# Perceiver block on one core: a cross product in two column tiles, its code sums on GpSimd

## The chip, the cores and the metric

The kernel runs on one core of a Trainium2 chip. The core has five engines that run side by side and wait for each other through semaphores: TensorE (PE, matrix products, with weight loads on their own track PEld), VectorE (DVE), ScalarE (ACT), GpSimd (POOL) and SyncE (SP, which here issues the DMAs). The metric is the device time of one execution in microseconds (us). The kernel before takes 621.97 us, the median of three runs (621.82 to 622.06).

## The reference

Sixteen batches of 64 rows of 1024 numbers pass through three residual steps. The first is the one that the change touches:

```
x = x + matmul(fake_quant(layernorm(x), s1, z1), fake_quant(ctx, s2, z2))   # ctx: 16 x 1024 x 1024
x = x + attention(layernorm(x))      # qkv, 32 heads, rope, causal softmax, output projection
x = x + ffn(layernorm(x))            # x W^T + bias + a sum of 16 low-rank updates
fake_quant(x, s, z) = (clip(round(x / s + z), 0, 255) - z) * s
```

With codes q1 and q2 (0 to 255) the product is s1 s2 times the sum over k of (q1 - z1)(q2 - z2). The kernel feeds TensorE q1 - 128 on one side and 1024 + q2 on the other, both exact in 16-bit floats. Two corrections remain: one per row of x, and one per column of ctx, which is (128 - z1) times the column's sum of codes.

## The kernel before

Two batches make a pair of 128 rows, so there are eight pairs. Pairs follow each other, and the cross product of pair i + 1 is worked into the attention of pair i. `next_pair` stands once for each engine (ACT, DVE, PE) and holds that engine's instructions for one such step in the order in which the engine runs them; pairs 2 to 5 or 6 run it in a loop, `first_pair` (pair 0), pair 1 and pair 6 or 7 are written out. No scheduler moves anything. Each engine works its own list in order, so an instruction that waits holds all that is behind it on that engine.

The ctx of a pair comes in 16 chunks of 128 x 1024 numbers (`CHUNKS`), chunk c being batch c // 8 and slice c % 8 of k. SP loads chunk c into one of three slots (`slots`: two of `raw`, and `lnt`), and it may load chunk c when chunk c - 3 has been read (`load_chunk`). ACT turns a chunk into codes (`quantise`): it writes the low bytes of a 16-bit tile in a ring of six (`code`, `RING`), whose high bytes were set once to the 1024. It waits until PE has used the chunk that had the slot (`s_cmm`). PE multiplies (`chunk`): the weights are 128 columns, 64 of q1 - 128 for this batch and 64 of ones (`q1t`), the streamed operand is 512 columns of codes, twice per chunk. So rows 0 to 63 of the bank pair `XX` hold the product of one batch and rows 64 to 127 the sums of its codes. DVE adds both to x with four instructions of 64 x 1024 per pair (`cross_evac`, two per batch, once after chunk 7 and once after chunk 15), then normalises (`norm2`); PE transposes the result (`x_turn`), which starts the next pair.

The places at which PE runs chunks, scores, transposes and the projection are the dictionaries in `next_pair`: `qkv(i, 1, {6: [at(c, 0)]})` runs chunk 0 after the seventh of eight steps of the second qkv block, each step being three products of 128 x 512. GpSimd issues the load of the rows after next (`rows_after_next`), does one addition of 128 x 1024, and is otherwise idle.

Of the kernel before, what the change touches and what calls it, by code (L numbers as in the profile page):

```python
# [36 lines left out]
RAW, RING = 2, 6  # L37
# [6 lines left out]
I32, U8T = mybir.dt.int32, mybir.dt.uint8  # L44
# [9 lines left out]
def build(nc, x, ctx_in, consts, qkv_w, out_w, bias_rows, out_bias, ffn_wt, ffn_bias, lora_a, lora_b, lora_w, out):  # L54
# [6 lines left out]
    with es:  # L61
# [14 lines left out]
        q1t = sb("q1t", [P, KC, 2, 2, SEQ], F16)  # L76
# [17 lines left out]
        qc = sb("qc", [P, 6], F32)  # L94
# [28 lines left out]
        d16 = pr[:, 0, :].bitcast(F16)  # L123
        s1, z1 = cst[:, C_SCAL:C_SCAL + 1], cst[:, C_SCAL + 1:C_SCAL + 2]
# [10 lines left out]
        q1v = q1t[:, :, :, :, :].rearrange("p k b h t -> p (k b h t)")  # L135
# [3 lines left out]
        lora_stage = [raw[:, 0, :], raw[:, 1, :], q1v.bitcast(F32), lnt[:, :]]  # L139
        wt_lnt = lnt[:, :].rearrange("p (u n) -> p u n", u=2)  # L140
        yn_h = [xn_h[:, :, :], q1v[:, 0:DM].rearrange("p (k t) -> p k t", k=KC)]
        yn_l = [xn_l[:, :, :], q1v[:, DM:2 * DM].rearrange("p (k t) -> p k t", k=KC)]
# [12 lines left out]
        s_ones = sem("s_ones")  # L155
# [28 lines left out]
        s_cmm = sem("s_cmm")  # L184
        s_clast = sem("s_clast")
# [125 lines left out]
        def _(act):  # L311
# [20 lines left out]
            def quantise(i, c):  # L332
# [25 lines left out]
            def a_high(i, e):  # L358
                act.wait_ge(s_at, 2 * i + e + 1)
                act.activation(q1t[:, 4 * e:4 * e + 4, :, 0, :],  # L360
                               code_bank(i, e)[:, :].rearrange("p (k b t) -> p k b t", k=4, b=2), ACT.Copy).then_inc(s_ah, 1)
# [7 lines left out]
            def v_evac(i, n):  # L369
                act.wait_ge(s_qkv, 6 * i + 5 + n)  # L370
                act.activation(vv[:, n * NT:(n + 1) * NT], D[n][:, :], ACT.Copy, scale=1.0 / (XSC * WSC)).then_inc(s_v, 1)

# [24 lines left out]
            def lora_high(n):  # L397
                act.wait_ge(s_lora[n], 16)
                if n == 0:
                    act.wait_ge(s_cmm, CHUNKS * PAIRS)  # L400
# [14 lines left out]
            def first_pair():  # L415
# [22 lines left out]
                exponent(0, 1)  # L438
                q(5, 6, 7, 8)
# [21 lines left out]
            def next_pair(i, more, late=False):  # L461
# [21 lines left out]
                q(7, 8)  # L483
                w(28)
                qk_evac(i, 1)
                q(9)
                w(29)
                q(10, 11)
                exponent(i, 0)
                q(12)  # L490
                exponent(i, 1)
                qk_evac(i, 2)
                q(13)
# [8 lines left out]
                q(14)  # L502
                w(31)
                if late:
                    v_evac(i, 0)
                    q(15)
                    exponent(i, 2)
                else:
                    exponent(i, 2)
# [83 lines left out]
        def _(sp):  # L593
            def load_chunk(i, c):
                if isinstance(i, int) and i == 0 and c == CHUNKS - 1:
                    for n in range(2):
                        sp.dma_start(chunk0_stage(c)[:, n, :], ctx_v[0, c // KC, c % KC, :, n * NT:(n + 1) * NT]).then_inc(s_clast if n else s_ctx0[c], 16)
# [1152 lines left out]
```

## Time and profile before

| | |
|---|---|
| median of the runs | 621.97 us |
| span of the profiled execution, from its first to its last instruction | 620.4 us |
| PE busy | 601.3 us (97%) |
| DVE busy | 472.8 us (76%) |
| ACT busy | 292.3 us (47%) |
| POOL busy | 11.5 us (2%) |
| one step of the pair loop, from one x_turn to the next | 58.25 us |

The span lies 1.57 us under the median of the runs; this is what lies around the span. A matmul's printed duration (0.38 us) holds its latency too. In a stream the starts stand 0.2155 us apart, and this spacing is what a product costs. Times in the rows are us from the start of the span; a bracket at a row's end is the time that the engine stood idle before it, and who ended that.

### The profile page before, as it was taken

The page shows a single profiled execution, that of the slowest core. Times are in us where ns is not written, and L with a number is a line of the kernel's source. Part 1 is how long each engine was busy: PE and PEld are TensorE (multiplying, and loading weights), DVE is VectorE, ACT ScalarE, POOL GpSimd, SP SyncE. Part 2 cuts the span into 40 slices and gives each one's busy share as a digit, 9 for nine tenths or more (in the row PEclk, how much of TensorE's full clock was granted, in tenths as well). Part 3 has the DMA queues.
Part 4 walks back from the last instruction along what each step waited for, and adds up shares of the span by engine and source line. Part 5 has one row for each costly group of instructions (what it writes and reads, how often), then busy time and mean ns, then how long its engine had stood idle before and what let it go on. Part 6 is the DMA issues. An engine that isn't in the chain of part 4 may idle for free.

```text
span 620.4 us, 12885 instructions
## 1 busy us (share of the span) xinstructions
PE 601.3 (97%) x4937; PEld 310.6 (50%) x4937; DVE 472.8 (76%) x938; ACT 292.3 (47%) x366; POOL 11.5 (2%) x17
## 2 busy tenths in 40 slices
PE   3898999999999999999999999999999999999998
PEld 1463454455455545554555455545545554454455
DVE  6899998788659965987596769659964789867661
ACT  5887695865464546534644554464431243110010
POOL 3000010000000000000000000000000000000000
PEclk9999999999999999999999999999999999999999
DMA  8999995861464175226712671464241042232311
GB/s 319 387 386 361 388 365 205 277 208 69 165 220 161 69 254 193 95 81 258 266 71 97 207 237 68 161 217 130 102 136 35 1 172 102 85 119 85 114 55 53
DMA packets 38912, 108.14 MB, mean 174 GB/s; under 512 B 3802, under 2 KB 4186, under 8 KB 38880
## 3 DMA queue, kind: packets, MB, share of 16 engines
q1 hardware_dynamic: 37744, 104.35, 47.5%
q0 software_dynamic: 992, 3.18, 1.5%
q8 instruction: 21, 0.34, 0.2%
q10 hardware_dynamic: 144, 0.18, 0.2%
q14 instruction: 11, 0.09, 0.0%
HBM read 99.30 MB, written 8.39 MB: 174 GB/s over the span
## 4 chain that ended last, share of the span: by engine, by line
PE 84%; DVE 5%; SPq 4%; DMA 4%; ACT 1%; issue 1%; ACTq 0%; DVEq 0%
PE dense L1259 16%; PE dense L1261 16%; PE dense L1260 16%; PE cross L1308 7%; PE turn L1250 6%; PE dense L1426 4%; PE dense L1427 4%; PE dense L1428 4%; DVE wq L860 4%; PE score L1387 2%; SPq L600 2%; DMA wq<-in_qkv_w 2%; PE score L1413 2%; DMA raw<-in_ctx 2%; PE dense L1442 1%; PE cross L1473 1%
## 5 line engine op out<-in xcount | busy, mean ns | idle before, releaser
L1259 PE MATMUL dense<-wq,xn_h 128*128 128x512 f16 x400 | 151.9, 380 | 0.0
L1260 PE MATMUL dense<-wq,xn_h 128*128 128x512 f16 x400 | 151.6, 379 | 0.0
L1261 PE MATMUL dense<-wq,xn_l 128*128 128x512 f16 x400 | 151.6, 379 | 0.0
L351 ACT ACTIVATE code<-raw,cst,qc 128x1024 uint8<-128x1024 f32 x72 | 87.7, 1235 | 6.7 <-DMA raw<-in_ctx 6.5
L1308 PE MATMUL cross<-code,q1t 128*128 128x512 f16 x256 | 73.4, 387 | 3.0 <-DVE xa L867 1.4
L1261 PEld LDWEIGHTS dense<-wq,xn_l 128*128 128x128 f16 x400 | 39.1, 98 | 47.2
L1259 PEld LDWEIGHTS dense<-wq,xn_h 128*128 128x128 f16 x400 | 39.1, 98 | 41.5 <-issue 1.6
L1260 PEld LDWEIGHTS dense<-wq,xn_h 128*128 128x128 f16 x400 | 39.2, 98 | 38.2
L351 ACT ACTIVATE code<-lnt,cst,qc 128x1024 uint8<-128x1024 f32 x32 | 39.6, 1239 | 28.4 <-DMA lnt<-in_ctx 25.4
L906 DVE SCALAR_TENSOR_TENSOR at<-cst,score 128x512 f32<-128x512 f16 x24 | 16.4, 683 | 37.4 <-PE score L1387 37.2
L1426 PE MATMUL dense<-wo,rope 128*128 128x512 f16 x112 | 42.5, 379 | 0.0
L1428 PE MATMUL dense<-wo,rope 128*128 128x512 f16 x112 | 42.4, 379 | 0.0
L1427 PE MATMUL dense<-wo,rope 128*128 128x512 f16 x112 | 42.4, 379 | 0.0
L1308 PEld LDWEIGHTS cross<-code,q1t 128*128 128x128 f16 x256 | 24.6, 99 | 33.8 <-ACT code L351 4.3
L367 ACT ACTIVATE at<-turn 128x512 f32<-128x512 f32 x32 | 19.0, 593 | 47.2 <-PE turn L1250 34.1
L381 ACT ACTIVATE at<-turn 128x512 f32<-128x512 f32 x32 | 19.1, 596 | 35.6 <-PE turn L1250 35.5
L375 ACT ACTIVATE at<-at 128x512 f32<-128x512 f32 x32 | 19.9, 624 | 32.2 <-DVE at L912 32.2
L892 DVE TENSOR_TENSOR rope<-dense,cst 128x512 f32<-128x512 f32 x32 | 22.0, 687 | 10.3 <-PE dense L1261 8.3
L943 DVE SCALAR_TENSOR_TENSOR xa<-dense,xa 128x512 f32<-128x512 f32 x16 | 11.0, 689 | 18.1 <-PE dense L1428 18.1
L387 ACT ACTIVATE rope<-score 128x256 f16<-128x256 f32 x28 | 9.2, 381 | 29.8 <-PE score L1413 29.8
L898 DVE TENSOR_TENSOR rope<-rope 128x512 f32<-128x512 f32 x32 | 22.1, 692 | 1.5
L920 DVE TENSOR_TENSOR at<-at,ssum 128x512 f32<-128x512 f32 x32 | 22.1, 692 | 1.1
(204 smaller groups left out, 992.6 us busy)
## 6 DMA issues: line engine op xcount, KB each, us to landing
raw<-in_ctx SPq DMA_DIRECT2D x72, 512.0 KB, 4.5
lnt<-in_ctx SPq DMA_DIRECT2D x32, 512.0 KB, 4.2
wo<-in_ctx SPq DMA_DIRECT2D x16, 512.0 KB, 8.6
wo<-in_qkv_w SPq DMA_DIRECT2D x12, 512.0 KB, 11.7
wq<-in_qkv_w SPq DMA_DIRECT2D x8, 512.0 KB, 11.9
x_scratch<-xa SPq DMA_DIRECT2D x8, 512.0 KB, 3.0
wq<-x_scratch SPq DMA_DIRECT2D x8, 512.0 KB, 3.7
wq<-in_ctx SPq DMA_DIRECT2D x7, 512.0 KB, 11.7
```

What stands on the lines that cost most here:

```text
L351: act.activation(low_bytes, src, ACT.Identity, scale=qc[:, 1:2], bias=z2).then_inc(s_u8, 1)
L860: dve.scalar_tensor_tensor(lo, staged(j), WSC, hi, ALU.mult, ALU.subtract).then_inc(s_wlo, 1)
L898: dve.tensor_tensor(rope[:, 2 + j % 2, :], rope[:, 0, :], rope[:, 1, :], ALU.add).then_inc(s_qr, 1)
L920: dve.tensor_tensor(p3, p3, ssum[:, g % 2, :].unsqueeze(2).to_broadcast([P, HPG, SEQ]), ALU.mult).then_inc(s_p, 1)
L1250: ins = pe.transpose(bank[:, k * P:(k + 1) * P], src[:, c:c + P], ident)
L1259: pe.matmul(bank[:, :], a_h[:, k, :], w_hi, start=(k == 0 and not started), stop=False)
L1260: pe.matmul(bank[:, :], a_h[:, k, :], w_lo, start=False, stop=False)
L1261: ins = pe.matmul(bank[:, :], a_l[:, k, :], w_hi, start=False, stop=(k == KC - 1 and not last))
L1308: ins = pe.matmul(X[n][:, :], lhs, code[:, c % RING, n * NT:(n + 1) * NT], start=(kc == 0), stop=(kc == KC - 1))
L1426: pe.matmul(D[n][:, :], c_h[:, k, :], wo_h[:, k, cols], start=(k == 0), stop=False)
L1427: pe.matmul(D[n][:, :], c_h[:, k, :], wo_l[:, k, cols], start=False, stop=False)
L1428: ins = pe.matmul(D[n][:, :], c_l[:, k, :], wo_h[:, k, cols], start=False, stop=(k == KC - 1))
```

## The change

- The products. PE no longer has columns of ones in the weights. For each slice kc of k it loads 64 columns of q1 - 128 per batch and runs the two batches as two matmuls into the two halves of the same bank (rows 0 to 63 and 64 to 127), first for columns 0 to 511, then for the others (`cross`). A chunk is now slice c // 2 of batch c % 2.
- The sums of codes. GpSimd adds each chunk's codes, as 32-bit integers that hold two codes each, to one of two accumulators (`add_codes`, 16 additions of 128 x 512 per pair). DVE casts both to 16-bit floats (`sums_as_f16`), and PE multiplies them by 128 - z1, as two 16-bit parts, in eight products into the same banks (`cross_shift`). For pair 0 PE takes the codes themselves with that shift (`first_cross`, six products more per slice).
- The addition to x. DVE reads each bank once, 128 x 512, two instructions per pair (`cross_evac`).
- The ring holds eight chunks. A slot is free when both PE and GpSimd have used it.
- The load of the rows after next is issued by ACT. The order in ACT's list and PE's list is written anew.

The core of the diff:

```diff
-RAW, RING = 2, 6
+CODE_SUM = -0x20032000
+RAW, RING = 2, 8
...
-                taken = CHUNKS * i + c - (CHUNKS % RING - 1 if c < CHUNKS % RING else RING - 1)
+                taken = CHUNKS * i + c - (RING - 1)
                 if above(taken):
                     act.wait_ge(s_cmm, taken)
+                if above(taken - CHUNKS):
+                    act.wait_ge(s_acc, taken - CHUNKS)
...
+            def add_codes(i, *cs):
+                for c in cs:
+                    pool.wait_ge(s_u8, CHUNKS * i + c + 1)
+                    if c < 2:
+                        pool.wait_ge(s_cbank, 2 * i)
+                        before = acc_from[:, :].to_broadcast([P, NT])
+                    else:
+                        pool.wait_ge(s_acc, CHUNKS * i + c - CHUNKS - 1)
+                        before = acc_words[:, c % 2, :]
+                    pool.tensor_tensor(acc_words[:, c % 2, :], code[:, c % RING, :].bitcast(I32), before, ALU.add).then_inc(s_acc, 1)
...
-                link(dve.scalar_tensor_tensor(x_rows(i)[rows, :], XX[0:SEQ, :], qc[0:SEQ, 2:3], x_rows(i)[rows, :], ALU.mult, ALU.add))
-                dve.scalar_tensor_tensor(x_rows(i)[rows, :], XX[SEQ:P, :], qc[SEQ:P, 2:3], x_rows(i)[rows, :], ALU.mult, ALU.add).then_inc(s_ce, 1)
+            def sums_as_f16(i):
+                dve.wait_ge(s_acc, CHUNKS * i)
+                dve.tensor_copy(acc[:, :], acc[:, :].bitcast(U16T)).then_inc(s_accf, 1)
+            def cross_evac(i, n):
+                dve.wait_ge(s_cbank, 2 * i + n + 1)
...
+                dve.scalar_tensor_tensor(x_rows(i)[:, cols], X[n][:, :], qc[:, 2:3], x_rows(i)[:, cols], ALU.mult, ALU.add).then_inc(s_ce, 1)
...
+            def cross(i, *ks):
+                for kc in ks:
...
+                    pe.wait_ge(s_u8, CHUNKS * i + 2 * kc + 2)
+                    for n in range(2):
+                        for b in range(2):
+                            ins = pe.matmul(X[n][b * SEQ:(b + 1) * SEQ, :], q1t[:, kc, b, :],
+                                            code[:, (2 * kc + b) % RING, n * NT:(n + 1) * NT], start=(kc == 0), stop=False)
+            def cross_shift(i):
+                pe.wait_ge(s_accf, i)
+                for n in range(2):
+                    for part in range(2):
+                        for b in range(2):
+                            ins = pe.matmul(X[n][b * SEQ:(b + 1) * SEQ, :], shift[:, part:part + 1].to_broadcast([P, SEQ]),
+                                            acc_sums[:, b, n * NT:(n + 1) * NT], start=False, stop=(part == 1))
...
-                    qkv(i, 1, {2: [at(codes)], 5: [at(codes_turned, 0), at(qk_turn, i, 0), at(m, 0)], 6: [at(c, 0)], 7: [at(c, 1)]})
+                    qkv(i, 1, {2: [at(codes)], 5: [at(codes_turned, 0), at(qk_turn, i, 0), at(m, 0)]})
...
-                    qkv(i, 4, {1: [at(turned, i, 2), at(p_turn, i, 0)], 4: [at(qk_turn, i, 3)], 6: [at(scores, i, 1)], 7: [at(p_turn, i, 1), at(c, 8, 9)]})
+                    qkv(i, 4, {1: [at(turned, i, 2), at(p_turn, i, 0)], 4: [at(qk_turn, i, 3)], 6: [at(scores, i, 1)], 7: [at(p_turn, i, 1), at(c, 4, 5)]})
...
-                qkv(i, 5, {1: [at(c, 10, 11), at(m, 4)], 2: [at(c, 12, 13), at(m, 5)], 3: [at(c, 14, 15), at(values_due, i, 0)], 4: [at(values, i, 0)],
-                           6: [at(evacuated, i, 0), at(p_turn, i, 2)], 7: [at(p_turn, i, 3)]})
+                qkv(i, 5, {1: [at(m, 4)], 2: [at(m, 5)], 3: [at(c, 6, 7), at(values_due, i, 0)], 4: [at(values, i, 0)],
+                           6: [at(shifted), at(evacuated, i, 0), at(p_turn, i, 2)], 7: [at(p_turn, i, 3)]})
```

In PE's new order slices 0 and 1 stand behind the first scores of the step, slices 2 and 3 in the fourth qkv block, 4 and 5 at the end of the fifth, 6 and 7 in the sixth.

ACT's list, in the copy of `next_pair` for pair 6 (the loop has the same order). `code<-` are the quantisations, `at<-at` the exponents of the softmax, `at<-turn` with `s_qkt` the copies of transposed q and k, `at<-turn` with `s_pt` the copies of transposed probabilities. Before, from chunk 12 of the next pair to its chunk 15:

```order
L351 ACTIVATE code<-raw,cst,qc 128x1024 [waits s_cmm,s_slot0]
L375 ACTIVATE at<-at 128x512 [waits s_sub]
L367 ACTIVATE at<-turn 128x512 [waits s_qkt]
L351 ACTIVATE code<-raw,cst,qc 128x1024 [waits s_cmm,s_slot1]
L381 ACTIVATE at<-turn 128x512 [waits s_pv,s_pt]
L367 ACTIVATE at<-turn 128x512 [waits s_qkt]
L381 ACTIVATE at<-turn 128x512 [waits s_pv,s_pt]
L351 ACTIVATE code<-lnt,cst,qc 128x1024 [waits s_cmm,s_slot2]
L375 ACTIVATE at<-at 128x512 [waits s_sub]
L351 ACTIVATE code<-raw,cst,qc 128x1024 [waits s_cmm,s_slot0]
L375 ACTIVATE at<-at 128x512 [waits s_sub]
```

Now, from the same exponent on (chunks 11, 12, 13, 14 and 15):

```order
L389 ACTIVATE at<-at 128x512 [waits s_sub]
L376 ACTIVATE at<-turn 128x512 [waits s_qkt]
L360 ACTIVATE code<-lnt,cst,qc 128x1024 [waits s_acc,s_cmm,s_slot2]
L395 ACTIVATE at<-turn 128x512 [waits s_pv,s_pt]
L376 ACTIVATE at<-turn 128x512 [waits s_qkt]
L395 ACTIVATE at<-turn 128x512 [waits s_pv,s_pt]
L360 ACTIVATE code<-raw,cst,qc 128x1024 [waits s_acc,s_cmm,s_slot0]
L360 ACTIVATE code<-raw,cst,qc 128x1024 [waits s_acc,s_cmm,s_slot1]
L360 ACTIVATE code<-lnt,cst,qc 128x1024 [waits s_acc,s_cmm,s_slot2]
L389 ACTIVATE at<-at 128x512 [waits s_sub]
L360 ACTIVATE code<-raw,cst,qc 128x1024 [waits s_acc,s_cmm,s_slot0]
L389 ACTIVATE at<-at 128x512 [waits s_sub]
```

Chunks 12 and 13 have moved behind the second copy of transposed probabilities; before, only 14 and 15 stood there.

DVE's list in the loop, from the third softmax to the rows that the projection needs (`at<-at,ssum` is a finished softmax, `rope<-score,rope` the low part of the attention's output). Now:

```order
L938 TENSOR_TENSOR at<-at,ssum 128x512 [waits s_dv]
L891 REGISTER_ALU
L892 CAST acc<-acc 128x2048 [waits s_acc]
L936 TENSOR_REDUCE ssum<-at 128x8 [waits s_exp]
L787 REGISTER_ALU
L937 RECIPROCAL ssum<-ssum 128x8 [waits s_dv]
L787 REGISTER_ALU
L938 TENSOR_TENSOR at<-at,ssum 128x512 [waits s_dv]
L896 REGISTER_ALU
L900 SCALAR_TENSOR_TENSOR xb<-cross,qc,xb 128x512 [waits s_cbank]
```

The cast, which waits for GpSimd's last addition, stands ahead of the fourth softmax; before, nothing stood between the third and the fourth.

## Rows read from the trace of the kernel before

**Rows 1.** The page: its span and the busiest engine.

```profile
span 620.4 us, 12885 instructions
PE 601.3 (97%) x4937; PEld 310.6 (50%) x4937; DVE 472.8 (76%) x938; ACT 292.3 (47%) x366; POOL 11.5 (2%) x17
```

**Rows 2.** Windows, loop step and pair 1: length, then PE, PEld, DVE, ACT, POOL busy.

```profile
276.00:334.25 58.25, 58.25 (x533) 30.12 (x532) 44.13 (x89) 29.23 (x36) 0.53 (x1) 1.00 0.46 162
...
103.28:159.28 56.00, 55.96 (x521) 28.62 (x519) 45.32 (x76) 37.00 (x45) 0.58 (x1) 1.00 0.51 170
```

**Rows 3.** PE's timeline in one loop step: start us, us, line, instruction, count.

```profile
292.02 0.61 PE L1250 MATMUL turn<-cst,rope 128*128 128x128 f32 x4
...
293.11 0.59 PE L1308 MATMUL cross<-code,q1t 128*128 128x512 f16 x2
293.54 0.38 PE L1259 MATMUL dense<-wq,xn_h 128*128 128x512 f16 x1
...
315.15 0.38 PE L1261 MATMUL dense<-wq,xn_l 128*128 128x512 f16 x1
315.46 1.16 PE L1387 MATMUL score<-at 32*64 32x64 f32 x64
...
317.21 0.60 PE L1250 MATMUL turn<-cst,at 128*128 128x128 f32 x4
...
322.83 1.03 PE L1308 MATMUL cross<-code,q1t 128*128 128x512 f16 x4
...
324.43 0.86 PE L1413 MATMUL score<-at 64*32 64x64 f32 x64
...
328.20 0.38 PE L1426 MATMUL dense<-wo,rope 128*128 128x512 f16 x1
```

**Rows 4.** ACT's timeline in the same loop step.

```profile
280.68 1.24 ACT L351 ACTIVATE code<-lnt,cst,qc 128x1024 uint8<-128x1024 f32 x1 [2.93 <-DMA lnt<-in_ctx]
...
317.85 0.60 ACT L381 ACTIVATE at<-turn 128x512 f32<-128x512 f32 x1 [2.98 <-PE turn L1250]
318.34 1.23 ACT L351 ACTIVATE code<-lnt,cst,qc 128x1024 uint8<-128x1024 f32 x1
...
319.99 1.23 ACT L351 ACTIVATE code<-raw,cst,qc 128x1024 uint8<-128x1024 f32 x1
```

**Rows 5.** SP's timeline: the issue of the load that ACT awaits at 280.68.

```profile
277.35 0.33 SPq L622 DMA_DIRECT2D lnt<-in_ctx  x1
```

**Rows 6.** DVE's timeline: a 16-bit scaling at the start, then the loop step.

```profile
25.41 0.48 DVE L1099 TENSOR_SCALAR rope<-rope,cst 128x1024 f16<-128x1024 f16 x1
...
285.31 0.16 DVE L783 SCALAR_TENSOR_TENSOR nw<-nw 128x1 f32<-128x1 f32 x1
...
291.22 0.69 DVE L898 TENSOR_TENSOR rope<-rope 128x512 f32<-128x512 f32 x1
...
323.94 0.69 DVE L920 TENSOR_TENSOR at<-at,ssum 128x512 f32<-128x512 f32 x1
324.67 1.28 DVE L866 SCALAR_TENSOR_TENSOR xb<-cross,qc,xb 64x1024 f32<-64x1024 f32 x1
...
327.30 0.76 DVE L936 SCALAR_TENSOR_TENSOR rope<-score,rope 128x256 f16<-128x256 f32 x2
```

**Rows 7.** GpSimd's one addition (POOL's timeline), and DVE beside it.

```profile
81.29 2.36 POOL L747 TENSOR_TENSOR xa<-xa,outb 128x1024 f32<-128x1024 f32 x1 [7.43 <-DVE at L920]
...
81.45 1.27 DVE L866 SCALAR_TENSOR_TENSOR xb<-cross,qc,xb 64x1024 f32<-64x1024 f32 x1 [0.33 <-PE cross L1308]
```

**Rows 8.** PE's timeline at the end of pair 0: the last chunk and x_turn.

```profile
94.83 0.60 PE L1308 MATMUL cross<-code,q1t 128*128 128x512 f16 x2 [0.26 <-ACT code L351]
...
103.12 1.04 PE L1250 MATMUL turn<-cst,lnt 128*128 128x128 f32 x8
```

**Rows 9.** DVE's and ACT's timelines at the start: last addition to x, first copy after x_turn.

```profile
32.22 0.76 DVE L878 SCALAR_TENSOR_TENSOR xa<-cross,qc,xa 64x512 f32<-64x512 f32 x1
...
38.91 1.07 ACT L355 ACTIVATE xn_h<-turn 128x512 f16<-128x512 f32 x2
```

More of the change, by code:

```diff
@@ L747, in _ @@
             pool.tensor_tensor(xa[:, :], xa[:, :], outb[:, :], ALU.add).then_inc(s_cp, 1)
-            with pool.Fori(1, PAIRS - 2) as i:
-                rows_after_next(i)
+            add_codes(1, *range(12, CHUNKS))
+            with pool.Fori(2, PAIRS) as i:
+                add_codes(i, *range(CHUNKS))
             pool.wait_ge(s_st, 16 * PAIRS)
@@ L813, in row_codes @@
                 dve.wait_ge(s_a, i + 1)
-                link(dve.tensor_scalar(rs1[:, :], rs1[:, :], qc[:, 3:4], qc[:, 4:5], ALU.mult, ALU.add))
+                constant = qc[:, 4:5] if isinstance(i, int) and i == 0 else qc[:, 6:7]
+                link(dve.tensor_scalar(rs1[:, :], rs1[:, :], qc[:, 3:4], constant, ALU.mult, ALU.add))
             def out_base(i):
@@ new lines, in cross_shift, with first_cross @@
+            def cross_shift(i):
+                pe.wait_ge(s_accf, i)
+                for n in range(2):
+                    for part in range(2):
+                        for b in range(2):
+                            ins = pe.matmul(X[n][b * SEQ:(b + 1) * SEQ, :], shift[:, part:part + 1].to_broadcast([P, SEQ]),
+                                            acc_sums[:, b, n * NT:(n + 1) * NT], start=False, stop=(part == 1))
+                    ins.then_inc(s_cbank, 1)
+            def first_cross(kc):
+                if kc == 0:
+                    pe.wait_ge(s_ah, 2)
+                pe.wait_ge(s_u8, 2 * kc + 2)
+                for n in range(2):
+                    if n and kc == KC - 1:
+                        pe.wait_ge(s_u8half, 2)
+                    for part in range(3):
+                        for b in range(2):
+                            lhs = q1t[:, kc, b, :] if part == 0 else shift[:, part - 1:part].to_broadcast([P, SEQ])
+                            ins = pe.matmul(X[n][b * SEQ:(b + 1) * SEQ, :], lhs, code[:, (2 * kc + b) % RING, n * NT:(n + 1) * NT],
+                                            start=(kc == 0 and part == 0), stop=(kc == KC - 1 and part == 2))
+                            if n and part == 2 and (b or kc < KC - 1):
+                                ins.then_inc(s_cmm, 2 if kc == KC - 1 else 1)
+                            elif part == 2 and kc == KC - 1 and b != n:
+                                ins.then_inc(s_cbank, 1)
@@ L1540, in first_pair, with c @@
             def first_pair():
-                def c(*cs):
-                    for n in cs:
-                        chunk(1, n)
+                def c(*ks):
+                    cross(1, *ks)
                 def rows_high(k):
@@ L1579, in next_pair, with c, shifted @@
             def next_pair(i, ahead):
-                def c(*cs):
-                    for n in cs:
-                        if ahead:
-                            chunk(i + 1, n)
+                def c(*ks):
+                    if ahead:
+                        cross(i + 1, *ks)
+                def shifted():
+                    if ahead:
+                        cross_shift(i + 1)
                 def m(u):
@@ L1628, in _ @@
             next_codes(0)
-            pe.wait_ge(s_ones, 1)
-            for n in range(CHUNKS):
-                chunk(0, n)
-                if n < KC:
-                    constants(16 if n == KC - 1 else 3)
+            for kc in range(KC):
+                first_cross(kc)
+                if kc < KC - 1:
+                    constants(6)
             next_codes(1)
```

151 lines of the change are left out of this document (71 added, 80 removed).

## The prediction

> **What bounds the kernel now.** I read first the page's busy shares: PE has something in flight for 601 of 620.4 us [rows 1]. That alone doesn't say that PE is the bound, so I read next the windows of one loop step: PE is busy for all of its 58.25 us, and for 55.96 of pair 1's 56.00 [rows 2]. Five of the eight pairs run such a step, so in the body of the kernel what leaves PE's list leaves the time, as long as nobody else becomes late. The third reading is therefore how close the others are, in the timelines of PE, ACT and DVE for one step [rows 3, 4, 6]. ACT sleeps 2.98 us before the copy at 317.85, since it waits for PE's transposition; its last code of the next pair starts at 319.99 and ends at 321.22, 1.6 us before PE takes chunks 14 and 15 (322.83). DVE ends the low part of the attention's output at 328.06, and PE's projection starts at 328.20. So ACT's margin for the last code is 1.6 us, and DVE's before the projection is 0.1.
>
> **The products.** A chunk costs PE 293.54 - 293.11 = 0.43 us [rows 3], sixteen cost 6.9 a pair. Now 32 matmuls run as 16 pairs of column tiles. If a pair costs one spacing of 0.2155, that is 3.45, and the eight shift products 0.86. That two column tiles with different streams do overlap, rows 3 bear out: at 324.43, 64 products of 64 f32 columns, in 2 row groups and 4 column groups, take 0.86 us. The four f32 transpositions of 128 columns at 292.02 are printed with 0.61, of which 0.17 is latency (a product's 0.38 less its spacing): 0.11 each. So 64 f32 columns cost 0.055, and one after another these 64 would take 3.5. Two row groups explain a factor of 2, the observed one is 4. Each change between full and tiled products costs a gap: scores start 0.31 after the product ahead of them (315.15 to 315.46), 0.1 over the spacing. Five tiled groups a step make 0.5. PE's list thus shrinks by 6.9 - 3.45 - 0.86 - 0.5 = 2.05 us a step. This is what a step would gain if nothing became late.
>
> The Trainium skill (TensorE: Matmul & The Clock Gate, Part 3) has three column tiles at 2.38 times one, 0.79 of the ideal; by that, as an estimate, a pair would cost 0.27 instead of 0.2155 and the sum below would rise by some 4 us.
>
> **The addition to x.** Four DVE instructions of 1.28 to 1.29 go (5.2 us a step, [rows 6]), two of 128 x 512 (0.69 at 291.22, some 0.65 from start to start) and the cast come: DVE has less to do.
>
> **GpSimd's additions.** One of 128 x 1024 takes 2.36 [rows 7]; half the columns, 1.2. Sixteen make 19 of 58 us, so GpSimd keeps pace; what counts is the last one, between the last code and the cast. **The cast** covers 2048 columns with 16 bits in and out. Nearest is the 16-bit scaling of 1024 in 0.48 [rows 6]: about 0.75. At one column per cycle, as DVE's two-input 512 columns in 0.69 minus a fixed 0.15 go, it would be 2.3. I take 0.75 since types and place agree, and keep 2.3 for the range.
>
> **Where the gain goes: the last code.** I follow one step in the clock of rows 3. Six chunks stood ahead of the first scores; none does now, so PE comes to them 2.6 us earlier. DVE and ACT follow, as their work there waits for PE. Then slices 0 to 3 (0.96 each two, with the gap) stand ahead of the second transposed probabilities, where chunks 6 and 7 (0.86) stood. That transposition moves from 317.21 to 317.21 - 2.6 + 1.92 - 0.86 = 315.66. ACT copies it 0.64 later and is free after 0.49, as in 317.85 to 318.34 [rows 4], at 316.8. Only then come the codes of chunks 12 and 13, of 1.23 each. Chunk 12 is done at 318.0; the load of chunk 15 into its slot waits for exactly that. A load of this size took from 277.35 to 280.68, 3.3 us, with an empty queue ahead of it [rows 4, 5]. So chunk 15 is there at 321.5 and its code at 322.7. PE reaches slice 7, which needs it, by its own list at 322.83 - 2.6 - 3.45 + 2.88 + 0.53 = 320.2 (the old place of chunk 14, less the six chunks, less chunks 6 to 13, plus three groups of 0.96, plus slice 6 and its gap). It waits 2.6 us, more than the step had gained.
>
> Before, this path was hidden, since chunk 12 was coded long before the copy at 317.85. Now two ends run from 322.7. PE: slice 7, the rest of the block, the values, the shift's products, two transpositions: 0.1 + 0.43 + 0.65 + 0.9 + 1.3 + 0.96 + 0.44 + 0.65 + 0.44 + 0.1 = 6.0, so the projection at 328.7. DVE: GpSimd's addition 1.3, cast 0.85 with its wait, fourth softmax 1.56 (its last instruction is the kind at 323.94), then PE's shift for bank 0 (there at 326.8), two additions 1.25, low part 0.76: 328.95. Against 328.20 the step is **0.75 us longer**. With a cast of 2.3 it is 1.95; with the load at 3.0 and no gaps 0.3. Behind the projection both have the work that they had, so the step ends later by this.
>
> **The sum.** Five loop steps: +3.75 (1.5 to 10). Pair 1: ACT's list has both copies of probabilities earlier, and the same walk brings the last code at 145.3, with PE at its slice at 145.1: of the 2.05 most stays, and GpSimd, cast and DVE take some back: -1.2 (-1.8 to -0.6). Pair 0: the last code is set by ACT and its loads and stays (PE waits for it at 94.83 already [rows 8]); behind it now follow GpSimd, cast, shift and the normalisation, and x_turn moves from 103.12 by +1.1 (0.8 to 1.5). Start: `first_cross` has 96 matmuls, 48 pairs instead of 32 singles, and PE ends near 33 instead of 30. DVE's last addition before ended at 32.98 [rows 9]; two of 0.65 behind PE's end make 33.7. x_turn is then 0.75 later, but ACT's copy stood at 38.91 behind a weight, 0.8 after x_turn's first half, which covers most: +0.3 (0 to 1). Four constant instructions more on DVE and a longer fill of the ring (8/6 of it) go under the first load. The issue of the rows on ACT costs about 0.4 in its idle time. The sum is +4.0, made against the profiled execution; what lies around its span (1.57 us) doesn't change. 621.97 + 4.0 = **626.0**.
>
> **Rivals.** *The last code is not late* (ACT or the load is quicker than I read, or PE's list is later anyway). Then each of six steps gains 2.05: 622.0 - 12.3 + 1.4 = 611. For it speaks that PE bounds every step now; against it the order of ACT's list, which no speed undoes. *GpSimd holds up DVE.* GpSimd's additions of chunks 3 and 4 fall on the chain of small two-input DVE instructions at 285.31, which leads to the transposition at 292.02, and that starts 0.1 after DVE's 291.91 [rows 3, 6]. If such an instruction had to wait for the running addition, up to 1.0 a step would be added: +5, 631. The one overlap in the trace doesn't show it: beside GpSimd's addition DVE's 1.27 is as long as elsewhere [rows 7, 6], but that instruction has only one input in SBUF. The Trainium skill (SBUF — State Buffer, Who interferes with whom) has it that a DVE instruction with two SBUF inputs and a GpSimd one that reads SBUF exclude each other; no row here tests it. *The tiles don't overlap.* Each slice then costs 0.86; a step is 3.7 longer and the start 10: 655. Rows 3 speak against it. *Slower sizes*: a cast of 2.3 and additions twice as long give +3 a step: 637.
>
> **Chances.** Late last code at the sizes above, 622.5 to 630: 0.52. GpSimd in DVE's way or slower sizes, 628 to 637: 0.23. The stall and the gain cancel, within 1.2 us of 622: 0.09. Not late, 608 to 620.5: 0.12. No overlap: 0.04. A measurement here tells about 0.2%, 1.2 us, from no change. Faster by more: 0.13; within: 0.10; slower: 0.77. The range leaves out the rival without lateness below and the last above: 619.5 to 637.
>
> **What would show it.** Right: in a loop step PE stands idle 2 to 3 us before the second last pair of slices' products, ended by ACT's code; ACT's chunk 15 waits for its load; the step is 59.0 us; x_turn of pair 1 stands near 104.4. Wrong: no idle PE there and a step of 56.2; or DVE's small instructions stretched to a microsecond beside GpSimd's; or tiled products 0.2155 apart one by one.

## The result, and the profile after

The changed kernel takes **652.5 us** (651.3 to 653.3) against 621.9: 1.049 times the kernel before, 95% interval 1.048 to 1.050. I had said 626.0, with 637 as the upper end. The direction was right, the size was not: +30.6 us in place of +4.

The page of the profiled execution of after, its first parts (us busy, share, instructions; then tenths in 40 slices):

```profile
span 651.5 us, 13443 instructions
PE 609.6 (94%) x5062; PEld 301.7 (46%) x5062; DVE 485.4 (75%) x929; ACT 290.4 (45%) x366; POOL 158.9 (24%) x124
...
PEclk9999979989999899989999999999899999999999
```

Beside [rows 1]: PE no longer fills the span, DVE is busy for 13 us more although two instructions of 0.75 us and a cast of 0.69 a step stand where four of 1.28 were, and the granted clock has dents. The waits of PE on others, summed over the span (total us, times, longest):

```profile
PE cross L1326 <- ACT code L360: 12.0, 5, 2.6
PE turn L1362 <- DVE at L838: 7.8, 6, 4.4
PE dense L1566 <- DVE wq L887: 6.2, 4, 3.1
...
PE turn L1274 <- DVE rope L916: 2.4, 1, 2.4
```

The first is the last code, and the others are waits for DVE (4.4 of the second stand at the kernel's start, where the kernel before has one of 3.6). The stages, from one x_turn to the next (busy us of PE, PEld, DVE, ACT, POOL; then granted clock):

```profile
41.10:113.50 72.40, 63.91 (x519) 28.80 (x517) 64.08 (x94) 49.81 (x59) 29.01 (x19) 0.95 0.81 299
113.50:172.30 58.80, 56.32 (x527) 27.26 (x528) 49.61 (x75) 36.79 (x45) 21.40 (x16) 0.97 0.48 162
172.30:236.00 63.70, 59.19 (x543) 28.84 (x542) 47.27 (x89) 29.84 (x38) 20.80 (x16) 0.97 0.43 149
236.00:297.80 61.80, 58.75 (x541) 28.60 (x540) 45.49 (x88) 29.09 (x36) 20.69 (x16) 0.97 0.44 153
297.80:358.80 61.00, 57.43 (x541) 28.23 (x540) 45.92 (x88) 29.05 (x36) 20.69 (x16) 1.00 0.45 155
```

Compare the loop step and pair 1 of [rows 2], both at a granted clock of 1.00. The table gives the lengths of all stages, read from the starts of x_turn in the timelines of PE (us; the runs are described below).

| run | x_turn of pair 0 | pair 0 | pair 1 | pair 2 | pairs 3 to 6 | median |
|---|---|---|---|---|---|---|
| before | 37.3 | 65.9 | 56.0 | 58.7 | 58.2 each | 621.9 |
| after | 41.1 | 72.4 | 58.8 | 63.7 | 61.8, 61.0, 61.9, 61.1 | 652.5 |
| codes_first | 39.4 | 71.8 | 59.5 | 59.7 | 58.1, 58.2, 58.0, 57.2 | 633.4 |
| no_sums | 40.3 | 68.5 | 54.5 | 61.4 | 61.0, 61.2, 61.1, 59.3 | 636.4 |
| both | 40.0 | 67.1 | 54.6 | 57.4 | 57.1, 57.1, 57.1, 57.0 | 619.5 |
| filler | 41.2 | 72.5 | 58.9 | 62.1 | 60.9, 60.5, 60.7, 59.8 | 646.2 |
| hold_sums | 40.0 | 72.2 | 54.6 | 58.2 | 57.9, 57.9, 57.9, 57.8 | 628.1 |
| sums_on_before | 36.9 | 71.3 | 56.2 | 62.6 | 60.9, 60.0, 60.9, 59.9 | 640.2 |
| mixed | 37.3 | 66.1 | 54.5 | 58.2 | 57.8 each | 619.4 |

So the 31.1 us by which the span grew are +3.8 at the start, +6.5 in pair 0, +2.8 in pair 1 and +17.9 in the five steps behind; pair 7 and the last stage are unchanged. The start is the least certain of these: among the profiles of the runs with the same list there, x_turn of pair 0 stands anywhere from 39.3 to 41.2, so its share is 2 to 4 us.

**The last code** is late as forecast. ACT in a loop step of after, then SP's load of chunk 15, then PE at the wait:

```profile
277.38 0.60 ACT L395 ACTIVATE at<-turn 128x512 f32<-128x512 f32 x1 [2.98 <-PE turn L1274]
277.87 2.36 ACT L360 ACTIVATE code<-raw,cst,qc 128x1024 uint8<-128x1024 f32 x2
...
282.74 1.24 ACT L360 ACTIVATE code<-raw,cst,qc 128x1024 uint8<-128x1024 f32 x1 [0.85 <-DMA raw<-in_ctx]
```
```profile
279.27 0.33 SPq L639 DMA_DIRECT2D raw<-in_ctx  x1
```
```profile
284.03 1.01 PE L1326 MATMUL cross<-code,q1t 128*64 128x512 f16 x4 [2.46 <-ACT code L360]
284.97 0.61 PE L1283 MATMUL dense<-wq,xn_h 128*128 128x512 f16 x1
285.37 0.63 PE L1284 MATMUL dense<-wq,xn_h 128*128 128x512 f16 x1
285.80 0.63 PE L1285 MATMUL dense<-wq,xn_l 128*128 128x512 f16 x1
...
346.38 0.62 PE L1326 MATMUL cross<-code,q1t 128*64 128x512 f16 x4 [2.56 <-ACT code L360]
346.94 0.39 PE L1283 MATMUL dense<-wq,xn_h 128*128 128x512 f16 x1
347.16 0.38 PE L1284 MATMUL dense<-wq,xn_h 128*128 128x512 f16 x1
```

ACT waits for the copy of the second probabilities, codes chunks 12 and 13, and SP's load of chunk 15 starts when chunk 12 is done; its code starts 3.5 us later. PE stands still for 2.46. What I had not put into the sum is in the starts behind that wait: 284.97, 285.37, 285.80 stand 0.40 to 0.43 us apart, twice the 0.2155 of a stream. The granted clock in 284 to 288 is 0.57, that is, mostly the lower of the two levels, 1.2 GHz. In the next step the wait of 2.56 is followed by full speed. From the wait's end to the projection the same work takes 291.77 - 284.03 = 7.74 us in the one and 352.76 - 346.38 = 6.38 in the other. Four of the five steps go like the first (granted clock 0.97 over the step), one like the second (1.00).

**GpSimd and DVE.** Groups of DVE by shape: after, then the run without GpSimd's additions, then the run in which GpSimd only writes (mean ns behind the busy time):

```profile
L916 DVE TENSOR_TENSOR rope<-rope 128x512 f32<-128x512 f32 x32 | 29.3, 916 | 1.4
L930 DVE TENSOR_TENSOR at<-at,smx 128x512 f32<-128x512 f32 x24 | 24.5, 1019 | 0.8
L927 DVE TENSOR_REDUCE smx<-at 128x8 f32<-128x512 f32 x24 | 16.5, 686 | 0.8
L809 DVE SCALAR_TENSOR_TENSOR nw<-nw 128x1 f32<-128x1 f32 x60 | 20.0, 333 | 2.1
L887 DVE SCALAR_TENSOR_TENSOR wo<-wo 128x1024 f16<-128x1024 f32 x7 | 11.2, 1597 | 3.7 <-ACT wo L337 3.7
```
```profile
L911 DVE TENSOR_TENSOR rope<-rope 128x512 f32<-128x512 f32 x32 | 22.1, 692 | 1.4
L925 DVE TENSOR_TENSOR at<-at,smx 128x512 f32<-128x512 f32 x24 | 16.6, 692 | 0.8
L804 DVE SCALAR_TENSOR_TENSOR nw<-nw 128x1 f32<-128x1 f32 x60 | 9.5, 159 | 2.1
```
```profile
L918 DVE TENSOR_TENSOR rope<-rope 128x512 f32<-128x512 f32 x32 | 22.1, 692 | 1.5
L932 DVE TENSOR_TENSOR at<-at,smx 128x512 f32<-128x512 f32 x24 | 16.6, 692 | 0.8
L811 DVE SCALAR_TENSOR_TENSOR nw<-nw 128x1 f32<-128x1 f32 x60 | 9.5, 159 | 2.1
```

Instructions with two inputs in SBUF are stretched in after (692 to 1019 ns, 159 to 333), the reduction with one input beside them isn't (686), and without GpSimd's reading all are back at the lengths of before [rows 6].

Pairs 0 and 1 pay most: without the additions (no_sums) they are 3.9 and 4.3 us shorter. In pair 0 DVE has its densest list. It computes the low parts of the weights (1.13 us apart when undisturbed), GpSimd adds beside it. DVE and POOL of after in pair 0, then PE, which waits for the low parts:

```profile
70.05 2.35 DVE L887 SCALAR_TENSOR_TENSOR wq<-at,wq 128x1024 f16<-128x1024 f32 x2
72.32 2.06 DVE L887 SCALAR_TENSOR_TENSOR wq<-spare,wq 128x1024 f16<-128x1024 f32 x1
74.31 4.50 DVE L887 SCALAR_TENSOR_TENSOR wq<-wo,wq 128x1024 f16<-128x1024 f32 x2
```
```profile
71.67 1.62 POOL L759 TENSOR_TENSOR acc<-code,acc_from 128x512 int32<-128x512 int32 x1 [2.60 <-ACT code L360]
73.84 3.89 POOL L759 TENSOR_TENSOR acc<-code,acc 128x512 int32<-128x512 int32 x2 [0.54 <-ACT code L360]
```
```profile
82.64 0.55 PE L1566 MATMUL dense<-wq,xn_h 128*128 128x512 f16 x1 [3.07 <-DVE wq L887]
84.85 0.61 PE L1566 MATMUL dense<-wq,xn_h 128*128 128x512 f16 x1 [1.66 <-DVE wq L887]
```

The lengths fit engines that take turns. GpSimd's first addition, 1.04 us alone, takes 1.62 and ends at 73.29, 0.9 behind the end of DVE's two at 72.40. DVE's next, 1.13 alone, takes 2.06 and ends at 74.38, 1.1 behind that.

Behind these waits of PE the granted clock falls too: it is 0.57 on average from 82 to 90 us, so part of pair 0's loss is clock. In pair 1 PE waits 2.4 us for DVE's rotation (the last line of the waits above), and from 134 to 136 the granted clock is 0.50. Without GpSimd's additions neither pair has such a dent.

### The profile page after: what moved, and what is told of

Same layout as the page of the kernel before. It is cut to its first block, busy times and chain, and to the rows that moved or that the text cites. A ratio compares the mean times of both kernels' runs of the same rounds, so it can differ in the third digit from the quotient of the medians.

```text
span 651.5 us, 13443 instructions
## 1 busy us (share of the span) xinstructions
PE 609.6 (94%) x5062; PEld 301.7 (46%) x5062; DVE 485.4 (75%) x929; ACT 290.4 (45%) x366; POOL 158.9 (24%) x124
## 4 chain that ended last, share of the span: by engine, by line
PE 72%; DVE 17%; issue 4%; DMA 3%; ACT 3%; DVEq 0%; ACTq 0%; SPq 0%
PE dense L1283 13%; PE dense L1284 12%; PE dense L1285 12%; PE turn L1274 6%; DVE wq L887 4%; PE dense L1473 4%; PE dense L1475 4%; PE dense L1474 4%; PE cross L1326 3%; DMA raw<-in_ctx 3%; PE score L1434 3%; ACT code L360 2%; PE cross L1352 2%; PE score L1460 2%; PE turn L1579 2%
## 5 line engine op out<-in xcount | busy, mean ns | idle before, releaser
L759 POOL TENSOR_TENSOR acc<-code,acc 128x512 int32<-128x512 int32 x98 | 134.6, 1391 | 203.7 <-ACT code L360 203.7
L1283 PE MATMUL dense<-wq,xn_h 128*128 128x512 f16 x400 | 154.0, 385 | 0.0
L1284 PE MATMUL dense<-wq,xn_h 128*128 128x512 f16 x400 | 153.5, 384 | 0.0
L1285 PE MATMUL dense<-wq,xn_l 128*128 128x512 f16 x400 | 153.4, 383 | 0.0
L1283 PEld LDWEIGHTS dense<-wq,xn_h 128*128 128x128 f16 x400 | 39.2, 98 | 50.1 <-issue 13.8
L1284 PEld LDWEIGHTS dense<-wq,xn_h 128*128 128x128 f16 x400 | 39.4, 99 | 35.6 <-issue 0.6
L1326 PE MATMUL cross<-code,q1t 128*64 128x512 f16 x224 | 32.6, 402 | 12.0 <-ACT code L360 12.0
L759 POOL TENSOR_TENSOR acc<-code,acc_from 128x512 int32<-128x512 int32 x14 | 15.2, 1084 | 105.9 <-ACT code L360 105.9
L395 ACT ACTIVATE at<-turn 128x512 f32<-128x512 f32 x32 | 19.1, 597 | 45.9 <-PE turn L1274 45.9
L916 DVE TENSOR_TENSOR rope<-rope 128x512 f32<-128x512 f32 x32 | 29.3, 916 | 1.4
L938 DVE TENSOR_TENSOR at<-at,ssum 128x512 f32<-128x512 f32 x32 | 26.2, 818 | 1.1
L930 DVE TENSOR_TENSOR at<-at,smx 128x512 f32<-128x512 f32 x24 | 24.5, 1019 | 0.8
```

Of the source, the lines that this page charges most:

```text
L759: pool.tensor_tensor(acc_words[:, c % 2, :], code[:, c % RING, :].bitcast(I32), before, ALU.add).then_inc(s_acc, 1)
L916: dve.tensor_tensor(rope[:, 2 + j % 2, :], rope[:, 0, :], rope[:, 1, :], ALU.add).then_inc(s_qr, 1)
L938: dve.tensor_tensor(p3, p3, ssum[:, g % 2, :].unsqueeze(2).to_broadcast([P, HPG, SEQ]), ALU.mult).then_inc(s_p, 1)
L1283: pe.matmul(bank[:, :], a_h[:, k, :], w_hi, start=(k == 0 and not started), stop=False)
L1284: pe.matmul(bank[:, :], a_h[:, k, :], w_lo, start=False, stop=False)
L1285: ins = pe.matmul(bank[:, :], a_l[:, k, :], w_hi, start=False, stop=(k == KC - 1 and not last))
```

## The experiments

Twelve kernels ran, each timed against the kernel before on its own chip. Theory A is the late last code with the clock behind it, theory B is GpSimd's additions in DVE's way.

**codes_first**: the codes of chunks 12 to 14 ahead of the copy.

```diff
                 else:
+                    q(12)
                     qk_evac(i, 3)
+                    q(13, 14)
                     p_evac(i, 1)
                 w(30)
-                q(12, 13)
+                if late:
+                    q(12, 13)
...
-                    q(14)
                     exponent(i, 2)
                     q(15)
```

> The changed kernel, with ScalarE's codes of chunks 12 to 14 moved ahead of the copy of the second transposed probabilities in the steps of pairs 2 to 6; nothing else. Theory A (the late last code costs the wait and the slow clock behind it): the 2.5 us in which TensorE waits for the last code go in all five steps, and with them the half clock behind the wait (some 1.4 us a step); steps of 57.5 to 58.2 us instead of 61 to 62, 634 us in all. Theory B (GpSimd in VectorE's way is the main cost, the wait only uncovers it): the wait moves to the sums' cast or the row chain, steps of 60 or more, 645 to 651.

633.4 us, ratio 1.0186 (1.0157 to 1.0215): 19.1 us less. PE's wait for a code is gone, loop steps are 57.2 to 58.2 at clock 1.00. In the profiles the five steps together are 18.3 us shorter, so nearly all of it is in the place that the edit touches. Pairs 0 and 1 stay long. A holds, and is not all.

**no_sums**: GpSimd's additions left out, and with them ACT's wait for them before it reuses a slot; the result lacks the zero point's shift.

```diff
-            add_codes(1, *range(12))
...
-            add_codes(1, *range(12, CHUNKS))
-            with pool.Fori(2, PAIRS) as i:
-                add_codes(i, *range(CHUNKS))
```

> The changed kernel without GpSimd's additions of the codes (the sums stay zero, so the zero point's shift is left out of the result; the cast and the eight products of the shift stay). Theory B: VectorE's instructions with two inputs in SBUF are back at their lengths (0.16, 0.69, 1.13 apart); pair 0 falls from 72.4 to about 66.5, pair 1 from 58.8 to 55 or 56, pair 2 by 2 and the later steps by 0.3 to 0.7: 638 us. Theory A alone: only the last addition's 1.3 us ahead of the cast goes, which nobody waits for: 650 to 652. Under both, TensorE's wait for the last code stays.

636.4 us, 1.0229 (1.0212 to 1.0246): 16.1 less. Pair 0 is shorter by 3.9, pair 1 by 4.3, pair 2 by 2.3; PE's wait for the last code stays (12.4 us in six waits). B holds too.

**both**: the two edits together.

> Both edits together: codes of chunks 12 to 14 earlier, and GpSimd's additions left out (the zero point's shift is missing from the result). If A and B are separate costs that add up: 652.5 - 18.5 - 14 = 620, with steps of 57 us and granted clock 1.00 throughout. If they overlap (one stall hides in the other), 624 or more.

619.5 us, 0.9964 (0.9950 to 0.9978): 33.0 less, where the single ones add up to 35.2. The two causes are nearly independent, and behind them nothing is left of the loss as a whole: steps are 1.1 shorter than before, the start and pair 0 still 2.7 and 1.3 longer. The granted clock has no dent.

**writes_only**: each addition of GpSimd replaced by a memset.

```diff
-                    pool.tensor_tensor(acc_words[:, c % 2, :], code[:, c % RING, :].bitcast(I32), before, ALU.add).then_inc(s_acc, 1)
+                    pool.tensor_tensor(tiny[:, c % 2:c % 2 + 1], acc_from[:, :], acc_from[:, :], ALU.add).then_inc(s_acc, 1)
+                    pool.memset(acc[:, c % 2 * DM:(c % 2 + 1) * DM], 0.0).then_inc(s_acc, 1)
```

> The changed kernel with each of GpSimd's additions of the codes replaced by a memset of half of the sums' buffer (1024 columns of 16 bits) behind a one-column addition that carries the wait: GpSimd writes SBUF for a similar time, but reads next to nothing of it (the zero point's shift is missing from the result). If it is GpSimd's reading that holds up VectorE's two-input instructions, they are as long as without additions, and the time is within 2 us of no_sums. If any running GpSimd instruction holds them up, the time stays above 648.

637.7 us, 1.0266 (1.0246 to 1.0287), 1.3 above no_sums. GpSimd is as busy as with additions (0.95 + 0.28 us each), and DVE's instructions have their old lengths (fence above). It is GpSimd's reading of SBUF that costs. ACT's wait for GpSimd is still in this run, so that wait isn't the price either.

**sums_on_before**: the additions put beside the kernel before, with ACT's wait for them and the load of the rows on ACT, but no tiles, no cast and no shift.

```diff
+                if above(taken - CHUNKS):
+                    act.wait_ge(s_acc, taken - CHUNKS)
...
+            def add_codes(i, *cs):
...
+                    pool.tensor_tensor(acc_words[:, c % 2, :], code[:, c % RING, :].bitcast(I32), before, ALU.add).then_inc(s_acc, 1)
```

> The kernel before, with GpSimd's sixteen additions a pair put beside it as they stand in the changed kernel (pairs 1 to 7); nobody uses the sums, a code's slot waits for its addition too, and the load of the next rows is issued by ScalarE as there. If the additions' price is their hold on VectorE, it is paid without column tiles, cast and shift as well: pair 0 some 5 us longer, pair 1 some 3, a later step 0.5 to 1.5, with VectorE's two-input instructions stretched: 632 to 638 us. If the price came from the sums' place ahead of the cast and the shift: 622 to 624.

640.2 us, 1.0294 (1.0269 to 1.0319): 18.6 more than before, a little over the range. Pair 0 pays 5.4, about as expected, pair 1 only 0.2, later steps 1.6 to 3.9. So the price needs neither tiles nor cast. I had the later steps too low: there DVE still has the four long additions to x, hence less slack, and in the five steps PE waits for it at the codes' transposition (3.2 us) and ahead of the projection (3.9). With 1.1 for the normalised probabilities these are 8.2 of the 12.6 us that the steps lose; the rest isn't placed. In pair 0 PE waits 3.1 for a code, behind which ACT had stood 4.87 us for DVE's softmax.

**filler**: eleven products of zero weights in the wait for the last code.

```diff
+                    if kc == KC - 1 and not isinstance(i, int):
+                        for _ in range(11):
+                            pe.matmul(X[0][0:SEQ, :], zcol[:, 0:1].to_broadcast([P, SEQ]), code[:, (2 * kc - 2) % RING, 0:NT], start=False, stop=False)
                     pe.wait_ge(s_u8, CHUNKS * i + 2 * kc + 2)
```

> The changed kernel, with eleven products of zero weights (0.2155 us each, 2.37 in all) put on TensorE between the seventh and the eighth slice in the steps of pairs 2 to 6, where it waits 2.46 us for the last code. They add nothing to the result. What the wait itself costs stays; only TensorE isn't idle in it. If the half clock behind the wait is a cost of its own, granted clock 1.00 in these steps, each 1.0 to 1.7 us shorter: 645 to 648 us. If it costs nothing because others are late by as much: 652.

646.2 us, 1.0381 (1.0363 to 1.0399): 6.3 less than after, for more work. All five steps have full clock, two of them here:

```profile
234.80:295.70 60.90, 59.80 (x553) 29.48 (x552) 46.03 (x88) 29.07 (x36) 20.68 (x16) 1.00 0.45 155
295.70:356.20 60.50, 59.79 (x553) 29.47 (x552) 45.65 (x88) 29.10 (x36) 20.73 (x16) 1.00 0.44 156
```

Of the 19.1 us of codes_first about a third is thus the clock behind the wait, the rest the wait itself (12.0 us in five steps of after).

**one_tile_at_a_time**: on `both`, the products of a group in the order of their tile.

```diff
-                for kc in ks:
...
-                    for n in range(2):
-                        for b in range(2):
+                for b in range(2):
+                    for kc in ks:
+                        for n in range(2):
```

> The run with both edits (codes earlier, no additions: the zero point's shift is missing from the result), with the cross products of a group put in the order of their column tile: all of batch 0, then all of batch 1, in place of taking turns. If products of two tiles now overlap and products of one tile can't, a group of two slices takes 1.51 instead of 0.86 us and a single slice 0.65 instead of 0.43: 2.6 us more in each step of pairs 1 to 6, 1.7 in pair 0, 619.5 + 17 = 636. If they don't overlap in either order (the rival of the prediction at 655): no change, 619.5.

619.0 us, 0.9954 (0.9938 to 0.9971): no change, against what I held for likely. Taken alone that would also fit tiles that don't overlap, so the next run was made.

**one_batch**: on `both`, batch 1's products left out, but for the first slice's.

```diff
-                        for b in range(2):
+                        for b in range(2 if kc == 0 else 1):
```

> The run with both edits (codes earlier, no additions), with batch 1's cross products left out but for the first slice's, so half of the products of pairs 1 to 7 are missing. If two column tiles run side by side, whatever their order in the list, the products left out were free: groups of two slices stay at about 1.07 us, steps at 57.1, 619.5 us. If a product of 64 columns simply costs half of one of 128 and they run one after another, a group falls by 0.43 us: steps of 55.4, 608 to 610 us.

619.3 us, 0.9961 (0.9948 to 0.9974): no change. PE in one step, a group of eight products in order of tile (one_tile_at_a_time), then a group of four of one tile alone (one_batch), each with the row behind it:

```profile
300.93 1.06 PE L1323 MATMUL cross<-code,q1t 128*64 128x512 f16 x8
301.92 0.39 PE L1280 MATMUL dense<-wq,xn_h 128*128 128x512 f16 x1
```
```profile
305.82 1.05 PE L1323 MATMUL cross<-code,q1t 128*64 128x512 f16 x4
306.80 0.39 PE L1280 MATMUL dense<-wq,xn_h 128*128 128x512 f16 x1
```

From start to start 0.99 us for eight products in two tiles and 0.98 for four in one: the second tile is free, also when its products stand behind all those of the first. The rival of tiles that don't overlap is out, though its 655 came nearest to the measured time.

**hold_sums**: on codes_first, GpSimd's additions from chunk 2 on wait for DVE's second rotation.

```diff
+                    if c == 2 and not isinstance(i, int):
+                        pool.wait_ge(s_qr, 4 * i - 2)
```

> The run with the codes of chunks 12 to 14 earlier, and in addition GpSimd's additions from chunk 2 on wait, in the steps of pairs 1 to 6, until VectorE has rotated the second block (the row chain ahead of the codes' transposition and the first two rotations are done by then). If the additions' hold on VectorE matters only through that chain: TensorE's waits for the row chain in the steps of pairs 2 to 5 (1.75, 0.56, 0.72 and 0.46 us) and for the rotation in pair 1 (3.4 us, with the half clock behind it) go, steps of 57.1 to 57.5, pair 1 at 55 to 56: 633.4 - 3.0 - 4.0 = 626.5 us. If the additions are only pushed onto a later part of VectorE's list that is as tight: 631 or more.

628.1 us, 1.0110 (1.0082 to 1.0138): 5.3 of the 7 expected. Pair 1 falls to 54.6 and PE's waits for the row chain in the steps are gone. A small new wait comes in their place (PE for the normalised probabilities, 2.2 us over six), since the additions now meet the softmax.

**short_warm** and **narrow_warm**: on codes_first, fewer or narrower products between `first_cross` and x_turn.

```diff
-WARM = 74
+WARM = 52
```
```diff
+                cols = 2 * SEQ if count == WARM else SEQ + P
...
-                    pe.matmul(T[0][:, 0:SEQ + P], row_of, c16[:, H_SEL:H_END], start=True, stop=True)
+                    pe.matmul(T[0][:, 0:cols], row_of, c16[:, H_SEL:H_SEL + cols], start=True, stop=True)
```

> The run with the codes of chunks 12 to 14 earlier, with 52 instead of 74 of the small products that keep TensorE busy between the first cross products and the transposition of pair 0's normalised rows. In all runs so far these 74 take 6.1 us behind the first cross products, and the transposition follows them at once, 1.8 us after VectorE has its first half ready. Theory: the transposition moves 1.8 us forward and with it the whole: 631.6 us. Rival (the weights' loads or VectorE's list set the stage behind it): no change, 633.4.

> The run with the codes of chunks 12 to 14 earlier, with the same 74 products ahead of the transposition of pair 0's rows as there, each 128 instead of 192 columns wide, so that TensorE's list keeps its length in instructions and takes 4.1 instead of 6.1 us. If the wait of 3.95 us without a releaser in the run with 52 products came from the shifted instructions, it is gone, the transposition of pair 0 is 1.8 us earlier than in the run with codes first, and the time is 631.6. If an earlier start makes pair 0 longer by itself: 636 or more. If the stage behind is set by something else: 633.4.

short_warm: 638.6 us, 1.0264 (1.0247 to 1.0281), slower by 5.2. x_turn is earlier (38.7), but pair 0 takes 79.0. PE in that stage:

```profile
91.05 1.15 PE L1436 MATMUL score<-at 32*64 32x64 f32 x62
96.15 0.47 PE L1436 MATMUL score<-at 32*64 32x64 f32 x2 [3.95 <-issue]
96.55 3.78 PE L1491 MATMUL dense<-wo,rope 128*128 128x512 f32 x4
```

Two of 64 products of one group come 3.95 us behind the others, with nothing in the profile that they waited for, and the clock behind is 0.50. narrow_warm, with as many instructions as codes_first, has no such wait: 632.2 us, 1.0163 (1.0148 to 1.0179), x_turn 39.2. There the narrower products take 4.3 us, so x_turn follows PE's list as read, but in this profile they start at 34.81, 1.5 later than in codes_first, and the time's interval overlaps that of codes_first: the gain of the whole is not shown.

A wait of this kind is not short_warm's alone. The same group of 64 products is broken by one in four other runs. PE in no_sums, behind 40 products of the group, and in one_batch, behind 46:

```profile
88.55 0.58 PE L1429 MATMUL score<-at 32*64 32x64 f32 x24 [1.38 <-issue]
```
```profile
88.12 0.56 PE L1431 MATMUL score<-at 32*64 32x64 f32 x18 [0.80 <-issue]
```

one_tile_at_a_time has 1.25 and writes_only 0.42, both behind the 40th. one_batch lacks six products ahead of this place and breaks at 46, short_warm lacks 22 and breaks at 62. So the wait belongs to one place in PE's list of instructions, not to the data. In no_sums it hides 1.4 us of what pair 0 gains.

**mixed**: pairs 0 and 1 by the products of before, the others by tiles, with both orders above.

```diff
+        q_ones = acc[:, :].rearrange("p (k b h t) -> p k b h t", k=KC, b=2, h=2)
...
-            add_codes(1, *range(12))
...
-            for kc in range(KC):
-                first_cross(kc)
...
+            for n in range(CHUNKS):
+                chunk(0, n)
```

> A version meant to beat both: pairs 0 and 1 (computed at the start and in pair 0's stage) have the products of the kernel before, with the ones beside the codes in one weight of 128 columns and no additions by GpSimd; pairs 2 to 7 have the column tiles, GpSimd's additions held until VectorE's second rotation, and the codes of chunks 12 to 14 earlier. By the costs found so far: start and pair 0 as before (transposition of pair 1's rows at 103.1 instead of 112), pair 1 54.6 and the later steps 57.8 to 58.1 as in the run with held additions: 618.5 us. Rival (pair 0's 6 us come from the ring of eight or the moved load, not from the additions): 624 or more.

**619.4 us**, 0.9960 (0.9946 to 0.9973): better than both kernels, by 0.4% against before. Pair 0 is back at 66.1, which leaves the ring of eight and the moved load without blame for pair 0; loop steps are 57.8.

## Why the prediction was wrong in size

The direction was right; two steps of the sum failed. It put the clock behind the new wait at nothing, and it put GpSimd's hold on DVE at nothing: that stood only as a rival, at 1.0 us a step and without pairs 0 and 1. For the five loop steps the profiles give the terms one by one. Products and additions to x gain 5.9 us (`both` against before), where I had five times 2.05. The late code costs 18.3 (after against codes_first), where I had five times 2.8 (the 2.05 that a step was to gain and the 0.75 that it was to grow). GpSimd's additions cost 5.5 (codes_first against `both`), where I had nothing. Together they make +17.9 in place of +3.75.

- **The last code: right.** Idle PE ahead of the last slice, ended by ACT's code, chunk 15 behind its load: forecast 2.6 us, measured 2.06 to 2.56 in the five steps. The load took 3.5 us in place of 3.3, and the copy released it as walked.
- **What stands behind it: the first error of the sum.** From slice 7 to the projection I put 6.0 us at full clock; it took 6.38 at full clock and 7.74 with the lower clock in its first 3.5 us. I treated a wait of PE as its own length. The kernel before never had one in the loop. Only its start shows the price: PE waits there for 5.76 and 3.61 us, and behind that two products take 0.80 us until about 20, then 0.43 (the view prints a granted clock of 1.00 for both):

```profile
14.95 1.01 PE L1308 MATMUL cross<-code,q1t 128*128 128x512 f16 x2 [0.79 <-issue]
15.75 0.69 PE L1532 MATMUL turn<-cst 128*128 128x192 f16 x3
...
20.11 0.59 PE L1308 MATMUL cross<-code,q1t 128*128 128x512 f16 x2
20.54 0.41 PE L1532 MATMUL turn<-cst 128*128 128x192 f16 x3
```

  The prediction drew on none of these rows. The filler puts 6.3 us on this.
- **GpSimd in DVE's way: the rival that came true, with a price too low.** I had it at 1.0 us a step, 631 in all, from the small instructions ahead of the codes' transposition. That place pays (L809 took 0.87 us once in a step instead of 0.16; PE waited 0.2 to 1.7 there), and for a loop step the price was right: 1.1 us by codes_first against `both`. But pair 0 and pair 1 I did not walk, and they pay 4.6 and 4.9 by the same two runs. By the windows of the kernel before, DVE is busy for 61.5 of pair 0's 65.8 us, with many two-input instructions of 1.13 us in a row, and sixteen additions fall on it. "Pair 0 +1.1" became +6.5, "pair 1 -1.2" became +2.8. Without the additions, in `both`, they are +1.3 and -1.4: the terms for the rest were right. All of this is 13.9 us beside early codes, 16.1 alone. The rule of the Trainium skill (SBUF — State Buffer, Who interferes with whom) that I had weighed, two SBUF inputs on DVE against a GpSimd instruction that reads SBUF, agrees with the 692 to 1019 ns, and with the 692 where GpSimd only writes. The row I had set against it had one input in SBUF and could not speak on this.
- **The products: overlap right, gap too small.** A second tile is free. But each group pays a change at both ends: 1.07 us for two slices from the stream's next slot to the next product, not 0.96. Five groups make 0.55. With the 0.15 that PE waits ahead of the projection, a step in `both` gains 1.15, not 2.05; 0.2 I can't place.
- **The start: the wrong bound.** I let DVE's addition set x_turn (+0.3, measured 2 to 4). It is PE's own list:

```profile
34.97 6.27 PE L1579 MATMUL turn<-cst 128*128 128x192 f16 x74
41.07 1.03 PE L1274 MATMUL turn<-cst,lnt 128*128 128x128 f32 x8
```
```profile
38.71 0.55 DVE L874 TENSOR_SCALAR lnt<-xa,mv,nw 128x512 f32<-128x512 f32 x1
```

  DVE has the first half ready at 39.26. The 74 small products that had filled 30.85 to 37.25 before now begin 4.1 us later and end 1.8 behind DVE. The list of PE was in front of me, and I had not read past `first_cross`.
- **The cast and the additions: right.** 0.69 us for the cast (0.75 said), 1.26 for an undisturbed addition (1.2).

Put together: 30.6 = 19.1 (late code, with its clock) + 13.9 (additions, with early codes) - 2.4 (`both` against before).

## What to carry to other kernels

Before work goes to an idle GpSimd, list DVE's two-input instructions in every stage, not in the loop alone, and count their time in the densest stage as if GpSimd's reading instructions stood in the same queue. A new wait of two microseconds on a PE that had none may cost half as much again in clock (here 6.3 us behind 12.0 of waits), so an order that avoids it (here three codes moved ahead of one copy, 19 us) comes before any gain in the products. And walk each engine's list to the end of the stage: filler sized for one schedule becomes the bound in the next (that taking it out pays, no run here shows).

## What the runs showed of the hardware

- GpSimd's instruction and DVE's two-input one lengthen each other when both read SBUF, and in pair 0 they fit taking turns: additions are 1.26 us alone, 1.39 on average and up to 2.25. Where GpSimd only writes, DVE's instructions keep their lengths (692 and 159 ns in writes_only).
- Two column tiles run side by side even when one tile's four products all stand ahead of the other's (0.99 us for eight, 0.98 for four of one tile). So the order within such a group is free.
- The lower clock comes behind some waits of 2.4 us and not behind others: 2.46 us at 281.6 was followed by it, 2.56 at 343.8 was not. I have no row that tells why.
- PE's wait without a releaser in pair 0 fits instructions that came late. It breaks the list at one place in five runs (behind 40 products, 46 with six fewer ahead, 62 with 22 fewer). In each, one packet of the queue for instructions moves some 2 to 3 us before the products go on, while data keep the 16 DMA engines full: from 84 to 85 us in writes_only and one_tile_at_a_time, 85 to 86 in one_batch, 86 to 87 in no_sums, 93 to 94 in short_warm (share of 100.5% by data in that last us). In after, codes_first, `both` and hold_sums, which have no such wait, it moves between 75 and 79, well ahead of the group. That PE waited for this packet is my reading; no run moves the load by itself, and why it came so late in short_warm, whose list is shorter, stays open. The 3.95 us and the lower clock behind them (0.50 from 96 to 100, 0.74 from 100 to 104, an estimate of 3 us) are the 7 us by which that stage is longer.
